# Retention inside a four-layer hybrid block: two of the gathered tiles are fetched and added at other places of the first stretch

## What is computed

```python
x = x + attn_a(layernorm(x))     # an RWKV time mix
x = x + ffn(layernorm(x))        # 64 experts, 4 choices for each token, and two shared experts
x = x + attn_b(layernorm(x))     # retention, 16 heads
x = x + ffn(layernorm(x))        # the same experts again
```

```python
q, k, v = x @ wq + bq, x @ wk + bk, x @ wv + bv            # split in 16 heads of 16
scores = einsum('bhnd,bhmd->bhnm', q, k) * dmask           # gamma ** (n - m) below the diagonal
ret = einsum('bhnm,bhmv->bhnv', scores, v)
norm = (ret - ret.mean((2, 3))) * rsqrt(ret.var((2, 3)) + eps)   # one mean and variance for each batch and head
out = silu(x @ wg + bg) * (norm * gn_w + gn_b) @ wo + bo
```

## Time and profile before

| | us |
|---|---|
| median of 3 timed runs | 1761.79 |
| lowest and highest of them | 1759.8, 1764.59 |
| span of the profiled execution | 1770.5 |
| POOL busy in it | 921.4 |
| DVE busy in it | 1091.4 |
| PE busy in it | 1348.5 |

### The profile page before, as it was taken

How to read it: one execution, slowest core, us unless ns; L and a number is a source line. 1 busy time by engine, 2 the same in 40 slices (tenths; PEclk the granted TensorE clock), 3 DMA queues, 4 the chain that set the end, 5 groups by cost and what they waited for, 6 DMA issues and landing times. The chain is left out here.

```text
span 1770.5 us, 24406 instructions
## 1 busy us (share of the span) xinstructions
PE 1348.5 (76%) x7408; PEld 924.2 (52%) x7408; DVE 1091.4 (62%) x2773; ACT 687.1 (39%) x1466; POOL 921.4 (52%) x1063
## 2 busy tenths in 40 slices
PE   6686656788699986998688985638876777777775
PEld 2344523455588873564456564325544555555533
DVE  5899755556366662473777775725654655555558
ACT  5998201111366652424133613111214444544420
POOL 3999364554555546656636032663453555555520
PEclk9898577889899998999799997869888888888878
DMA  9800531121788876112111003521136444443168
GB/s 363 343 1 0 201 136 56 71 86 61 207 276 265 271 250 185 57 46 69 39 53 39 3 1 128 219 101 49 68 97 185 148 140 140 140 134 105 40 238 272
DMA packets 109395, 233.81 MB, mean 132 GB/s; under 512 B 21543, under 2 KB 43470, under 8 KB 108756
## 3 DMA queue, kind: packets, MB, share of 16 engines
q1 hardware_dynamic: 81076, 164.03, 27.6%
q0 software_dynamic: 27648, 68.23, 11.3%
q10 hardware_dynamic: 544, 0.00, 0.0%
HBM read 125.44 MB, written 115.11 MB: 136 GB/s over the span
## 5 line engine op out<-in xcount | busy, mean ns | idle before, releaser
L882 POOL DMA_INDIRECT slots_x<-arena,slot x256 | 258.2, 1009 | 207.7 <-DVEq L981 131.4
L1248 POOL DMA_INDIRECT pairs_y<-arena x192 | 189.1, 985 | 177.2 <-DVE arena L1319 117.4
L1167 PE MATMUL moe_narrow<-arena 128*128 128x128 f32 x1536 | 232.7, 301 | 8.0 <-DVE arena L1311 6.7
L1311 DVE TENSOR_TENSOR arena<-arena,moe_narrow 64x128 f32<-64x128 f32 x384 | 111.6, 291 | 205.2 <-ACT arena L1215 186.3
L1167 PEld LDWEIGHTS moe_narrow<-arena 128*128 128x128 f32 x1536 | 212.9, 215 | 16.7 <-issue 15.0
L1156 PE MATMUL moe_narrow<-ident,arena 128*128 128x128 f32 x768 | 137.7, 308 | 92.8 <-ACT arena L1209 68.3
L707 PE MATMUL moe_wide<-arena 128*128 128x512 f32 x384 | 190.7, 644 | 22.0 <-DVE arena L1002 22.0
L1209 ACT ACTIVATE arena<-moe_narrow 128x512 f32<-128x512 f32 x192 | 114.6, 597 | 197.7 <-remote 117.8
L456 POOL DMA_INDIRECT arena<-slots_y,slot x128 | 128.7, 1005 | 87.0 <-DMA arena<-slots_y,slot 46.6
L1156 PEld LDWEIGHTS moe_narrow<-ident,arena 128*128 128x128 f32 x768 | 93.7, 155 | 146.8 <-issue 143.8
L799 ACT ACTIVATE arena<-moe_wide 128x512 f32<-128x512 f32 x48 | 28.7, 598 | 319.0 <-PE moe_wide L707 153.7
(11 more groups left out here) (318 smaller groups left out, 2410.4 us busy)
## 6 DMA issues: line engine op xcount, KB each, us to landing
arena<-slots_x SPq DMA_DIRECT2D x192, 264.0 KB, 3.8
slots_x<-arena SPq DMA_DIRECT2D x48, 528.0 KB, 15.8
slots_y<-arena SPq DMA_DIRECT2D x96, 256.0 KB, 3.7
arena<-w_gu SPq DMA_DIRECT2D x2, 8192.0 KB
arena<-pairs_y SPq DMA_DIRECT2D x32, 512.0 KB, 5.7
residual<-x SPq DMA_DIRECT2D x8, 512.0 KB
arena<-sw_gu SPq DMA_DIRECT2D x4, 1024.0 KB
slots_x<-arena,slot POOLq DMA_INDIRECT x256
```

Source lines behind the costliest of these rows:

```text
L882: pool.indirect_dma_start(out=x_slots, in_=xn[:, t, :], in_offset=None, out_offset=bass.IndirectOffsetOnAxis(ap=slot[:, t, i:i + 1], axis=0))\
L1167: last = pe.matmul(h_ps[n % 2][:, j * P:(j + 1) * P], weights[:, n % 3, j, h, :], xt[:, n % XTRING, (j * KH + h) * P:(j * KH + h + 1) * P] ...
L1248: pool.indirect_dma_start(out=slots.y_of, in_=ytile[:, n % YRING, j, :], in_offset=None, bounds_check=slots.pairs - 1, oob_is_err=False, o ...
```

## The change

In the first stretch, batch 2's tiles 4 and 5 are gathered after `add_output_bias(1)` and not before `group_power(0)`. Batch 2's tiles 2 and 3 are no longer added as a pair after `keep_values(1, 1)`: tile 2 is added alone before the variance, tile 3 alone in the middle of `output(0)`, by a new function `add_tile` in which each of four instructions waits for the one before. `statistics(2, 0)` moves behind `output(0)`. The other stretches keep their order, and no work is added or left out.

```diff
+    def add_tile(self, dve, t, turn, place):
+        k = self.k
+        tile = one_tile(k.res, t)
+        for i in range(self.K):
+            if i == 0:
+                for parity in range(2):
+                    dve.wait_ge(self.sem(f"in{place}_{parity}"), 16 * (self.K // 2) * (turn + 1))
+            else:
+                dve.wait_ge(self.sem("added"), self.K * (t - self.first) + i)
+            weight = k.gate[:, bass.ds(t, 1), i:i + 1].rearrange("p o i -> p (o i)")
+            dve.scalar_tensor_tensor(tile, self.ring[:, place, i, :], weight, tile, ALU.mult, ALU.add)\
+                .then_inc(self.sem("added"), 1)
...
                 layernorm_power(H * (b + 1) + 1)
                 if more:
-                    gather(b + 2, range(4 if b else 2, 6))
+                    gather(b + 2, range(4, 6) if b else range(2, 4))
                 group_power(b)
...
                 add_output_bias(b + 1)
+                if not b:
+                    gather(b + 2, range(4, 6))
...
-            def output(b):
+            def output(b, pairs=range(TB // 2)):
                 dve.wait_ge(sem("bias_added"), b + 1)
-                for i in range(TB // 2):
+                for i in pairs:
...
                     add_choices(b + 2, 0)
                     if b:
                         add_choices(b + 2, 1)
+                    else:
+                        add_tile(b + 2, 2)
...
                     variance(b)
                     gate(b)
                     keep_values(b + 1, 1)
-                    if not b:
-                        add_choices(b + 2, 1)
-                    statistics(b + 2, 0)
-                    output(b)
+                    if b:
+                        statistics(b + 2, 0)
+                        output(b)
+                    else:
+                        output(b, range(2))
+                        add_tile(b + 2, 3)
+                        output(b, range(2, TB // 2))
+                        statistics(b + 2, 0)
```

More of the change, by code:

```diff
@@ L2343, in add_choices, with add_tile @@
                 choices.add_pair(dve, TB // 2 * b + pair, TB // G * b + 2 * pair // G, 2 * pair % G)
+            def add_tile(b, t):
+                choices.add_tile(dve, TB * b + t, TB // G * b + t // G, t % G)
             def late_multiply(q):
```

## The result

The changed kernel took 1755.45 us in the median of 18 runs (1747.01 to 1761.94), the kernel before 1761.43 us in 18 runs beside them (1755.33 to 1773.57). The ratio is 0.9959, with a 95% interval of 0.9941 to 0.9976: 7.2 us faster by the ratio (4.2 to 10.4), 6.0 by the medians. The forecast was 8.6 us, 1753.2 us.

The account below looks back on a forecast made before the run. `gate` waits 11.4 us for POOL, busy with 16 gathers; slow additions follow. Of 18.9 us gained at chunks(1), POOL's longer queue takes part back, leaving 8.6 at `gate(1)`: 1761.8 - 8.6 = 1753.2 us, 8-in-10 range 1747.5 to 1759.

Parts of the forecast that it names:

- tile 2's four additions: First stretch, DVE before the variance: 1.6 to 3.3 us, hidden in 7.57 us of idle time.
- tile 3's four, under the decays: Middle of `output(0)`: four additions slowed by POOL's decays, 1.3 us each, 5.2 us in all.
- The wait that goes and the cover that comes with it: First stretch: `gate` starts 10.4 us earlier without gathers before `group_power(0)`; tile 2's addition fits DVE's idle time, costing nothing.
- The gathers that come back: Behind `add_output_bias(1)`: 32 gathers, not 24, at 1.62 us each make POOL the late one, `layernorm_power(5)` at 912.0.
- The stall: Among the 32 gathers: one caught in DVE's sixteen additions costs 2.8 us, sized from two cases of 3.5 and 2.1.
- The cold PE: Second stretch, `layernorm_power(5)` to variance: PE runs dry and falls to half clock; 1.0 us added to 15.8.
- The credit of up to 1 us for a PE that is free: Second stretch: the chain to the variance may be up to 1 us shorter, as PE is free when ACT delivers.
- POOL's queue at a pace of 1.96: Rival, chance 0.19: slower gathers before `layernorm_power(5)` take nearly all back; gain 0.5 us, 1761.3 us.
- the faster rival: Chance 0.15: the 32 gathers run at 1.55 us each or without the stall; at 1.55, gain 14.6 us, 1747.2 us.
- a later stretch moves as a block: From `gate(1)` on, the second stretch's end, chunks(2) and the last stretches all shift by the same 8.6 us.
- the additions' move as a term of the sum: First stretch: DVE's new order is counted with the moved gathers, bringing chunks(1) 18.9 us earlier.
- The eight gathers in front of `group_power(1)`: Second stretch: POOL's gathers of tiles 4 and 5 end at about 926.8, just ahead of the variance at 928.8.

Follow-up runs that it names:

- the change's other two traces: The changed kernel, unchanged, run and traced twice more against the kernel before: ratio 0.9947 where that takes 1762 us, 0.9971 where it takes 1533 us.
- both stretches: The change applied to the second stretch as well, against the kernel before: ratios 0.9892 and 0.9898, timed only on the faster kind of chip; median 1518.46 us.
- more in flight: The changed kernel with no gather waiting for the one two before it, against the kernel before on the faster kind: ratio 0.9875, 19.2 us faster.
- kernel before with more in flight: The kernel before with no gather waiting for the one two before it, against itself unedited on the slower kind: ratio 1.0231, 41 us slower.
- the second pair: Second traces of both kernels where the kernel before takes 1762 us: kernel before again, ratio 1.0006; changed kernel again, ratio 0.9947.
- the halves: Two kernels, each with one part of the change, against the kernel before: moved gathers only, 0.9991 and 0.9980; DVE's new order only, 0.9974 and 0.9968.
- the gathers alone: Only batch 2's gathers of tiles 4 and 5 moved, DVE's order as in the kernel before: ratios to it 0.9991 and 0.9980.
- the additions alone: Only DVE's order changed, all 16 gathers before `group_power(0)` as in the kernel before: ratios to it 0.9974 and 0.9968.

## Why the prediction was right

Each step by its own term, from the variance on (the prediction's times less 832.7):

| step | forecast | measured |
|---|---|---|
| gate(0) | 1.1 | 1.05 |
| tile 2's four additions | 1.6 to 3.3 us, hidden | 2.05 us, hidden |
| tile 3's four, under the decays | 5.2 us | 5.08 us |
| chunks(1), first mask | 19.7 | 18.8 |
| layernorm_power(4) | 19.5 | 18.3 |
| gathers restart | 24.7 | 23.5 |
| 32 gathers with one stall of 2.8 | 54.6 us | 54.1 us, one stall of 2.7 |
| layernorm_power(5) | 79.3, set by POOL | 77.6, set by POOL |
| from it to the variance | 16.8 us, with 1.0 for a cold PE | 17.4 us |
| gate(1) | 97.2 | 96.1 |
| gain there | 8.6 us | 9.6 us |
| gain in the timed runs | 8.6 us | 7.2 us (4.2 to 10.4) |

- *The wait that goes and the cover that comes with it* were right to a tenth of a microsecond. The page had nothing on them; the row of `gate`'s first instruction and POOL's order gave them.
- *The gathers that come back* were the step that decided the size. Reading the first stretch alone gives 19 us. The queue of 32 gathers at the pace of the same place, 1.62, and one stall gave it within 0.5 us. So close a match is partly luck: the same 32 gathers took 53.7 and 56.1 us in the change's other two traces. That this queue is the cause, and not only coincides, is shown by both stretches and by more in flight on one kind of chip: take the eight gathers out, or speed them up, and `layernorm_power(5)` comes 10 to 14 us earlier.
- *The stall* was sized from two cases. It recurs: in each of the eleven traces with two in flight at least one gather that met a group of sixteen additions took from 2.1 to 4.5 us. All fourteen traces together have 30 gathers of more than 1.4 us, and every one of them ends 0.81 to 0.84 us behind the last addition of a group that it met, as the two long ones of rows 10 do. So a stalled gather waits for the end of the additions, and its price is what is left of them. It doesn't need two in flight: in the kernel before with more in flight one took 4.05 us. But most gathers inside a group pass in 0.94 to 1.3 us, with two in flight and with more; which one is caught stays open. The rule of the Trainium skill that I weighed there (SBUF — State Buffer, its box on DVE blocking DMA) tells of a stall only for perf modes that these additions don't use; the traces show one all the same. In the kernel before with more in flight:

```profile
964.14 6.42 DVE L484 SCALAR_TENSOR_TENSOR residual<-arena,gate,residual 128x256 f32<-128x256 f32 x16
...
965.76 1.25 POOL L456 DMA_INDIRECT arena<-slots_y,slot  x1 [0.30 <-DVE residual L484]
967.32 4.05 POOL L456 DMA_INDIRECT arena<-slots_y,slot  x1 [0.30 <-issue]
```

- *The cold PE* was undersized: 1.0 us for what cost 1.7 net (17.4 against 15.8; 2.5 and 2.0 in the change's other two traces). The credit of up to 1 us for a PE that is free was right: with PE free and warm, in both stretches, the same way took 14.9 us, 0.9 less than before. It was the cold clock that cost more than the 1.9 of the prediction: 2.5 us against that, up to 3.4.
- *The rivals.* POOL's queue at a pace of 1.96 didn't come; the measured 54.2/32 is 1.69 with the stall; nor did the faster rival's 1.55 without one. That a later stretch moves as a block held in this pair of traces: 9.6 us at `gate(1)`, 8.5 at the end of retention. In the second pair it is 8.7 and 12.3, so the later stretches scatter by some us of their own.
- *The sums* have one slip: 849.5 and 2.6 for `statistics` make 852.1 for chunks(1), and 20.2 less 1.0 makes a gain of 19.2, not 852.4 and 18.9. It changes nothing behind it, since POOL's queue starts from `layernorm_power(4)`.
- *The size on the other kind of chip* is not the forecast's: there the change gained 4.4 us (2.0 to 6.9), though its `layernorm_power(5)` and `gate(1)` lie within 2.5 us of those on this kind. The kernel before has no trace there, so where the rest went stays open.
- *What was missed* is the weight of the halves. The prediction treats the additions' move as a term of the sum, 18.9 us where the gathers alone would give 10; by the halves' traces it is worth 0 to 3 us at `layernorm_power(5)`, and the moved gathers are worth as little once the additions are moved. The eight gathers in front of `group_power(1)`, which the prediction had just ahead of the variance (926.8 against 928.8), were what held `gate(1)` for 2.3 and 4.3 us with the additions alone.

## What to carry to other kernels

Issues taken out from in front of a wait go somewhere: add them to the queue in which they land, at the pace measured in that very place, before counting the gain of the stretch they left. When a queue turns out to be the next bound, move the same kind of work out of that place too; here, where all were timed, the second application brought 10 us and the first 4.4. And a version that issues faster must be timed on every chip it is to run on: more gathers in flight took the changed kernel from 4.4 to 19.2 us below the kernel before on one kind, and made the kernel before 41 us slower on the other. The changed kernel with more in flight was not run on the slower kind, nor the kernel before with it on the faster; the starved matmuls in the traces are what says that the kind, and not the kernel, makes the difference.

## What the runs showed of the hardware that was not expected

- Two kinds of chip, 13% apart on the same program: 1762 and 1534 us. Retention is nearly the same on both (gate(1) of the change at 96 and 98 us, end at 247 to 248); the difference lies in the phases around it. In the experts' phase the weight loads for the transposes were idle 148.4 us in the change's second trace, on the slower kind (136.3 in its first), and 65.6 on the faster, nearly all put down to "issue":

```profile
L1171 PEld LDWEIGHTS moe_narrow<-ident,arena 128*128 128x128 f32 x768 | 92.6, 153 | 148.4 <-issue 145.2 <-DMA arena<-slots_x 3.1
```
```profile
L1171 PEld LDWEIGHTS moe_narrow<-ident,arena 128*128 128x128 f32 x768 | 85.8, 145 | 65.6 <-issue 62.3 <-DMA arena<-slots_x 3.2
```

- PE can starve with no wait in the program when gathers of 128 rows are issued every 1.25 us: a matmul every 1 to 3 us in chunks on the slower kind of chip, with its clock at 0.50; with two in flight it doesn't. The same pace left it busy on the faster kind, and on the slower kind where its matmuls were few and long. It may be the same thing as the point above; no run tells.
- A gather's issue can take 4.45 us in place of 0.95: in all 30 cases above 1.4 us it lasted until 0.81 to 0.84 us behind the last of a group of DVE's additions. With more in flight there were two such cases in three traces (4.05 and 2.07 us), with two in flight 28 in eleven.
